# Second attention: VectorE adds GpSimd's pair sums once more; loads, normalising and table loads moved in the other stages

## What is computed

```python
x = x + attn_a(layernorm(x))   # 16 heads of 8, RoPE, heads mixed before and after the softmax
x = x + ffn(layernorm(x))      # 64 of 1024 tokens a sequence, picked by a router, go through a small block
x = x + attn_b(layernorm(x))   # 8 heads of 32, keys and values from a latent of 64
x = x + ffn(layernorm(x))

def attn_b(x):
    q = (x @ Wq.T); kv = x @ Wkv_down.T; k = kv @ Wk_up.T; v = kv @ Wv_up.T
    scores = einsum('bqhd,bkhd->bhqk', q, k) * 32 ** -0.5
    return einsum('bhqk,bkhd->bqhd', softmax(scores), v) @ Wo.T
```

## Time and profile before

| what | us |
|---|---|
| runs of the kernel (three) | 2303.29, 2316.74, 2319.06 |
| the profiled execution's own time | 2306.53 |
| its span, first to last instruction | 2304.7 |
| PE (TensorE matmuls) busy | 2070.8 (90%) |
| DVE (VectorE) busy | 1921.1 (83%) |
| ACT (ScalarE) busy | 1727.7 (75%) |
| POOL (GpSimd) busy | 874.3 (38%) |

### The profile page before, as it was taken

The page is one execution under the profiler, slowest core; times in us unless marked ns, Lnnn a source line. Parts: engine busy times, 40 slices in busy tenths (PEclk is TensorE's granted clock), DMA queues, the critical chain, the costliest instruction groups (busy, mean ns, idle before and its releaser), DMA issues. The chain is left out here.

```text
span 2304.7 us, 61585 instructions
## 1 busy us (share of the span) xinstructions
PE 2070.8 (90%) x24624; PEld 1439.3 (62%) x24624; DVE 1921.1 (83%) x2625; ACT 1727.7 (75%) x3059; POOL 874.3 (38%) x952
## 2 busy tenths in 40 slices
PE   5799999999999999999999999846679999999555
PEld 3477776777777777767777777644336666556454
DVE  6899999999999999999999999683658888888564
ACT  1699998999999899999999999522447777777322
POOL 3433232333332332323233233440028777777230
PEclk9999999999999999999999999956879999999866
DMA  2599999999999999999999999700221111110101
GB/s 100 97 193 197 196 194 194 193 199 193 195 197 195 195 195 195 193 195 193 194 196 199 190 197 195 127 27 0 90 91 31 30 30 33 34 30 23 37 1 37
DMA packets 1099199, 305.39 MB, mean 133 GB/s; under 512 B 1070753, under 2 KB 1092129, under 8 KB 1098657
## 3 DMA queue, kind: packets, MB, share of 16 engines
q1 hardware_dynamic: 1097760, 297.83, 74.6%
q10 hardware_dynamic: 1152, 3.62, 0.4%
HBM read 22.44 MB, written 10.49 MB: 14 GB/s over the span
## 5 line engine op out<-in xcount | busy, mean ns | idle before, releaser
L439 DVE SCALAR_TENSOR_TENSOR a_parts<-a_probs,a_parts 128x1024 f16<-128x1024 f32 x512 | 658.6, 1286 | 70.7 <-ACT a_parts L391 70.1
L350 PE MATMUL a_out_ps<-a_vs,a_pT 128*128 128x128 f16 x4096 | 712.3, 219 | 4.4 <-DMA a_pT<-a_parts 4.4
L354 PE MATMUL a_out_ps<-a_vs,a_pT 128*128 128x128 f16 x4096 | 712.2, 219 | 0.0
L352 PE MATMUL a_out_ps<-a_vs,a_pT 128*128 128x128 f16 x4096 | 712.2, 219 | 0.0
L383 ACT ACTIVATE a_probs<-a_score_ps,a_negmax 128x1024 f32<-128x1024 f32 x512 | 571.2, 1116 | 95.0 <-DVE a_negmax L433 86.6
L433 DVE TENSOR_REDUCE a_negmax<-a_score_ps 128x1 f32<-128x1024 f32 x512 | 621.6, 1214 | 12.2 <-PE a_score_ps L336 9.2
L493 POOL TENSOR_TENSOR a_weighed<-a_own_out,wpost 128x256 f32<-128x256 f32 x256 | 246.6, 963 | 956.5 <-DVE a_parts L439 951.6
L391 ACT ACTIVATE a_parts<-a_probs 128x1024 f16<-128x1024 f32 x512 | 540.2, 1055 | 25.7 <-DMA a_pT<-a_parts 25.1
L350 PEld LDWEIGHTS a_out_ps<-a_vs,a_pT 128*128 128x128 f16 x4096 | 400.7, 98 | 64.4 <-ACT a_own_out L401 4.0
L352 PEld LDWEIGHTS a_out_ps<-a_vs,a_pT 128*128 128x128 f16 x4096 | 400.7, 98 | 59.5
L332 PE MATMUL a_score_ps<-kh,a_qs 128*128 128x512 f16 x1024 | 390.2, 381 | 36.8 <-ACT a_probs L383 28.4
(11 more groups left out here) (199 smaller groups left out, 2217.6 us busy)
## 6 DMA issues: line engine op xcount, KB each, us to landing
a_pT<-a_parts SPq DMA_TRANSPOSE x512, 5.0
b_qs<-q_parts SPq DMA_DIRECT2D x96, 64.0 KB, 1.9
b_ks<-k_parts SPq DMA_DIRECT2D x96, 64.0 KB, 2.0
q_parts<-b_parts SPq DMA_DIRECT2D x32, 128.0 KB, 1.8
k_parts<-b_parts SPq DMA_DIRECT2D x32, 128.0 KB, 1.9
x<-x_dram SPq DMA_DIRECT2D x4, 512.0 KB, 11.9
a_rope<-rope_dram ACTq DMA_DIRECT2D x1, 2048.0 KB, 11.1
out_dram<-x SPq DMA_DIRECT2D x4, 512.0 KB, 5.3
```

What stands on the lines that cost most here:

```text
L350: pe.matmul(out[:, 0:D], hi, vs[:, b, 0, j, :], start=j == 0, stop=False, skip_group_check=True)
L352: pe.matmul(out[:, 0:D], hi, vs[:, b, 1, j, :], start=False, stop=False, skip_group_check=True)
L354: last = pe.matmul(out[:, 0:D], lo, vs[:, b, 0, j, :], start=False, stop=j == JB - 1, skip_group_check=True)
L439: dve.scalar_tensor_tensor(out=parts[:, T % RING_P, 1, :], in0=probs[:, T % RING_P, :], scalar=PSCALE, in1=parts[:, T % RING_P, 0, :], op0 ...
```

## The change

Six edits. (1) attend_b: a new tile quads; VectorE adds pair sums 0 and 1 (half 0) and 2 and 3 (half 1) of a unit, TensorE's ones products read the two results, so they are half as many. The sum of half 1 of unit u-1 stands first in VectorE's unit u, that of half 0 of unit u behind invert(u-1). GpSimd's pair sums wait for VectorE's sum two units before instead of for the products. (2) prepare_a: rope and wpost are loaded by SP behind x, TensorE no longer waits for them; VectorE normalises 8 tiles, ScalarE 24, four in each chunk. (3) The feed stages' weights and tables are loaded once, in project_a (class FeedWeights, held to the end), and no stage waits for them. (4) A square root of one column is taken by ScalarE at the start of project_a and project_b and at the end of the first picked_block. (5) picked_block: hnT is copied ahead of twice. (6) prepare_b: VectorE normalises 8 tiles first and four more behind each chunk's low parts.

```diff
@@ prepare_a @@
+        shift, shift_ready, normed_rest = st.sb(s, "a_shift", [P, NT]), st.sem("a_shift_ready"), st.sem("a_normed_rest")
-        LOADS = 8
+        LOADS = 6
...
                              io["x"][b].rearrange("(t p) d -> p t d", p=P)).then_inc(x_in[b], 16)
+            sp.dma_start(rope[:], io["rope"]).then_inc(rope_in, 16)
+            sp.dma_start(wpost[:], io["wpost"].broadcast_to([P, HA * D])).then_inc(wpost_in, 16)
...
-            act.dma_start(rope[:], io["rope"]).then_inc(w_in, 16)
             act.dma_start(wpre[:], io["wpre"]).then_inc(w_in, 16)
-            act.dma_start(wpost[:], io["wpost"].broadcast_to([P, HA * D])).then_inc(w_in, 16)
             layernorm_scalar(act, ln)
+            act.wait_ge(shift_ready, 1)
             for c in range(NCH + 2):
                 if c < NCH:
                     act.wait_ge(transposed, c + 1)
                     act.copy(hT[:, c * CH:(c + 1) * CH], tps[c % 2][:]).then_inc(hT_ready, 1)
+                if c + DVE_NORMED < NCH:
+                    for t in range(4 * (c + DVE_NORMED), 4 * (c + DVE_NORMED) + 4):
+                        act.activation(xn[:, t, :], x[:, t, :], ACT.Identity, bias=shift[:, t:t + 1],
+                                       scale=ln.rstd[:, t:t + 1]).then_inc(normed_rest, 1)
...
-            normalise(dve, ln, x)
+            dve.scalar_tensor_tensor(out=shift[:], in0=ln.mv[:, :, 0], scalar=-1.0, in1=ln.rstd[:], op0=ALU.mult,
+                                     op1=ALU.mult).then_inc(shift_ready, 1)
+            normalise(dve, ln, x, range(4 * DVE_NORMED))
             dve.wait_ge(w_in, 16 * LOADS)
+            dve.wait_ge(rope_in, 16)
@@ attend_b @@
+        quads = st.sb(s, "b_quads", [P, 2, 2, HALF])
...
-                pe.wait_ge(added, PAIRS * u + 2 * half + 2)
-                for pair in range(2 * half, 2 * half + 2):
-                    for t in range(TILES):
-                        last = pe.matmul(out_ps[t * HDB:(t + 1) * HDB, 0, P:], ones[:],
-                                         sums[:, u % 2, pair, t * P:(t + 1) * P], start=False,
-                                         stop=pair == PAIRS - 1, skip_group_check=True)
+                pe.wait_ge(quad_ready, 2 * u + half + 1)
+                for t in range(TILES):
+                    last = pe.matmul(out_ps[t * HDB:(t + 1) * HDB, 0, P:], ones[:],
+                                     quads[:, u % 2, half, t * P:(t + 1) * P], start=False, stop=half == 1,
+                                     skip_group_check=True)
                 last.then_inc(pv_done, 1)
...
+            def add_pairs(u, half):
+
+                if u < 0:
+                    return
+                dve.wait_ge(added, PAIRS * u + 2 * half + 2)
+                if u >= 2:
+                    dve.wait_ge(pv_done, 2 * (u - 2) + half + 1)
+                dve.tensor_tensor(quads[:, u % 2, half, :], sums[:, u % 2, 2 * half, :], sums[:, u % 2, 2 * half + 1, :],
+                                  ALU.add).then_inc(quad_ready, 1)
+
...
             for u in range(units):
+                add_pairs(u - 1, 1)
                 row_max(TILES * (u + 1) + 2)
                 row_max(TILES * (u + 1) + 3)
                 row_max(TILES * (u + 2))
                 invert(u - 1)
+                add_pairs(u, 0)
                 row_max(TILES * (u + 2) + 1)
+            add_pairs(units - 1, 1)
             invert(units - 1)
...
                 if u >= 2:
-                    pool.wait_ge(pv_done, 2 * (u - 2) + pair // 2 + 1)
+                    pool.wait_ge(quad_ready, 2 * (u - 2) + pair // 2 + 1)
@@ project_a @@
+        @block.sync
+        def _(sp):
+            for to, source in fw.sources:
+                sp.dma_start(to[:], source).then_inc(feed_in, 16)
+            sp.wait_ge(feed_in, 16 * len(fw.sources))
...
         def _(act):
+            act.wait_ge(w_in, 48)
+            act.activation(fw.warm[:], ident[:, 0:1], ACT.Sqrt)
@@ route @@
-        @block.sync
-        def _(sp):
-            sp.dma_start(wr[:], io["w_router"].broadcast_to([P, D])).then_inc(w_in, 16)
...
             add_eps(dve, ln)
+            dve.tensor_reduce(wsum[:], wr[:], AX.X, ALU.add, negate=True).then_inc(summed, 1)
             done = invert_root(dve, ln, 0)
...
-            dve.wait_ge(w_in, 64)
-            dve.tensor_reduce(wsum[:], wr[:], AX.X, ALU.add, negate=True).then_inc(summed, 1)
@@ picked_block @@
+            act.copy(hnT[:], A[:, 0:2 * QK].rearrange("p (r t) -> p r t", r=2)).then_inc(hnT_kept, 1)
             act.copy(twice[:], A[:, 0:2 * QK].rearrange("p (b t) -> p b t", b=NB)[:, :, None, :]
                      .broadcast_to([P, NB, 2, CAP])).then_inc(twice_kept, 1)
-            act.copy(hnT[:], A[:, 0:2 * QK].rearrange("p (r t) -> p r t", r=2)).then_inc(hnT_kept, 1)
...
+            if lnext:
+                act.activation(wts.warm[:], ident[:, 0:1], ACT.Sqrt)
@@ prepare_b @@
-            normalise(dve, ln, x)
+            normalise(dve, ln, x, range(8))
...
+                if c + 2 < NCH:
+                    normalise(dve, ln, x, range(4 * c + 8, 4 * c + 12))
@@ project_b @@
+        @block.scalar
+        def _(act):
+            act.activation(fw.warm[:], fw.ident[:, 0:1], ACT.Sqrt)
```

More of the change, by code:

```diff
@@ L32 @@
 GT_RING = 4
+DVE_NORMED = 2
 LN_EPS, RMS_EPS = 1e-5, 1e-6
@@ L125, in invert_root, with normalise @@
     return n + 5
-def normalise(dve, w, x):
-    for t in range(NT):
+def normalise(dve, w, x, tiles):
+    for t in tiles:
         dve.tensor_scalar(w.xn[:, t, :], x[:, t, :], w.mv[:, t, 0:1], w.rstd[:, t:t + 1],
@@ L208, in _ @@
                 if c < NCH:
-                    pe.wait_ge(ln.normed, 4 * c + 4)
+                    if c < DVE_NORMED:
+                        pe.wait_ge(ln.normed, 4 * c + 4)
+                    else:
+                        pe.wait_ge(normed_rest, 4 * (c - DVE_NORMED) + 4)
                     if c >= 2:
@@ L250, in _ @@
                                              op1=ALU.mult).then_inc(prod_ready, 1)
+            dve.wait_ge(wpost_in, 16)
         @block.gpsimd
@@ L779, in __init__, with project_a @@
         self.loaded = st.sem("pa_w_in")
-def project_a(st, x, acc, pw, lstats):
+def project_a(st, x, acc, pw, lstats, fw):
     nc = st.nc
@@ L846, in _, with route @@
             tile_moments(dve, lstats, taken, NCH - 1)
-def route(st, io, w, tag, x, xn, oh, ohT, xsel, xh, lstats):
+def route(st, w, tag, x, xn, oh, ohT, xsel, xh, lstats):
     nc = st.nc
@@ L855, in route @@
         ln = LnWork(st, s, tag + "ln", xn, lstats)
-        ident = st.sb(s, tag + "ident", [P, P])
-        wr = st.sb(s, tag + "wr", [P, D])
-        iota = st.sb(s, tag + "iota", [P, 2, 2 * CAP])
-        below = st.sb(s, tag + "below", [P, P])
+        ident, wr, iota, below = w.ident, w.wr, w.iota, w.below
         junk = st.sb(s, tag + "junk", [P, 4, P])
@@ L880, in route @@
         block = s.enter_context(nc.Block())
-        @block.sync
-        def _(sp):
-            sp.dma_start(wr[:], io["w_router"].broadcast_to([P, D])).then_inc(w_in, 16)
-            sp.dma_start(iota[:], io["iota"]).then_inc(w_in, 16)
-            sp.dma_start(below[:], io["below"]).then_inc(w_in, 16)
-            sp.dma_start(ident[:], io["ident"]).then_inc(w_in, 16)
-            for to, source in w.sources:
-                sp.dma_start(to[:], source).then_inc(w.loaded, 16)
         @block.scalar
@@ L987, in _ @@
         def _(pe):
-            pe.wait_ge(w_in, 64)
             pe.wait_ge(score_ready, 1)
@@ L1050, in _, with __init__ @@
             turn(NB - 1)
-class BlockWeights:
-    def __init__(self, st, stack, io, tag):
+class FeedWeights:
+    def __init__(self, st, stack, io):
         def sb(name, shape):
-            return st.sb(stack, tag + name, shape)
-        self.ident, self.g, self.wqkv = sb("ident2", [P, P]), sb("g", [P, 2, D]), sb("wqkv", [P, 3, D])
+            return st.sb(stack, "fw_" + name, shape)
+        self.ident, self.g, self.wqkv = sb("ident", [P, P]), sb("g", [P, 2, D]), sb("wqkv", [P, 3, D])
         self.wout, self.w12, self.w3 = sb("wout", [P, D]), sb("w12", [P, 2, 3 * P]), sb("w3", [P, 3, D])
         self.headm, self.pairm, self.causal = sb("headm", [P, HA]), sb("pairm", [P, D]), sb("causal", [P, CAP])
-        self.loaded = st.sem(tag + "w2_in")
-        self.sources = ((self.ident, io["ident"]), (self.g, io["g"].broadcast_to([P, 2, D])),
+        self.wr, self.iota, self.below = sb("wr", [P, D]), sb("iota", [P, 2, 2 * CAP]), sb("below", [P, P])
+        self.warm = sb("warm", [P, 1])
+        self.sources = ((self.ident, io["ident"]), (self.wr, io["w_router"].broadcast_to([P, D])),
+                        (self.iota, io["iota"]), (self.below, io["below"]),
+                        (self.g, io["g"].broadcast_to([P, 2, D])),
                         (self.wqkv, io["fqkv_T"]), (self.wout, io["fout_T"]), (self.w12, io["w12_T"]),
@@ L1295, in _, with feed_forward @@
                 last.then_inc(put_done, 1)
-def feed_forward(st, io, tag, x, lstats, lnext):
```

(10 more changed lines are left out.)

18 lines of the change are left out of this document (7 added, 11 removed).

## The result

| | before | after |
|---|---|---|
| time, median (lowest to highest) | 2310.93 us (2303.29 to 2319.06, 4 runs) | 2507.02 us (2505.49 to 2507.65, 4 runs) |
| span of the profiled execution | 2304.7 us | 2505.5 us |
| granted TensorE clock, mean | 0.946 | 0.915 |

What follows compares the result with a forecast made beforehand. It took a ring through VectorE's new sum in the second attention, 8.86 us a unit, as the bound: 2304.7 + 123 - 8.5 - 5.1 = 2414.1 of span, 2416 us in time, range 2346 to 2445.

Steps and rivals of the forecast that it cites:

- Second attention, +123: attend_b: 60 units growing from 6.84 to 8.86 us, 121 us, plus about 1.2 and 0.6 us at the end.
- The ring: attend_b: half 1's sum delays a row maximum, TensorE, the next exponentials and so its own next inputs; 8.86 us a unit.
- collision: attend_b: VectorE's sum of half 1 waits for GpSimd's next pair sum on the shared SBUF port; 1.00 us a unit.
- the rival: attend_b: VectorE's sum doesn't wait for GpSimd's pair sum; unit 7.86 us, +63 us, total 2356; chance 0.17.
- the rival on the granted clock: attend_b: TensorE's idle time drops it to half clock; 12.8 us units, a quarter of 60 adding 59 us, 2475; chance 0.12.
- the likeliest case: Whole kernel: 2416 us, own range 2400 to 2430, attend_b units of 8.86 us at clock 1.00; chance 0.66.
- the 3.45 us of the ring: attend_b: from L586 through scores, exponentials and scaled maxima to the next exponential 6, 3.45 us a unit at full clock.
- the units could alternate: attend_b: by the skill's loop that falls to the low clock every round, units could alternate between clocks; no size given.
- The second sum: attend_b: VectorE's sum of half 0, behind the reciprocal, costs nothing; up to 1 us if it met a GpSimd sum.
- Loads and normalising, -8.5: Ahead of the first attention: statistics end near 13 us, 9.1 earlier, less 0.2 and 0.3; bounds -5 and -9.5.
- Small stages, -5.1: Feed stages and projections: table loads -1.7 and +0.5, router weights' DMA wait -2.9, later copy -1.0.
- The wait for the root: Both feed stages: VectorE's 2.3 us wait behind the table load falls to about 0.3 each, -1.7 over both.

Runs made afterwards that it cites:

- experiment 3: Changed kernel plus 18 unread 256-column matmuls filling TensorE's idle stretch in each unit of the second attention: 2419.46 us, ratio 1.0461.
- experiment 2: Changed kernel, but GpSimd's first pair sum of a unit waits until VectorE's sum of half 1 of the unit before is done: 2353.8 us, ratio 1.019.
- experiment 7: Changed kernel with first row maximum ahead of half 1's sum: 2296.77 us; same with old prepare_a: 2306.61; changed kernel with old attend_b: 2293.89.
- e2: The kernel before with only the changed attend_b: 2514.4 us, ratio 1.0884.
- e11: Changed kernel with the next unit's first row maximum ahead of the sum of half 1, and prepare_a as before the change: 2306.61 us, ratio 0.9979.
- experiment 4: Changed kernel plus unread matmuls in TensorE's idle stretch, fewer than 18: with 7, 2418.89 us, ratio 1.0452; with 3, 2488.49 us, one run.
- e6: Changed kernel, first row maximum ahead of the sum of half 1, and GpSimd's next pair sum waiting for that sum: 2296.15 us, ratio 0.992.

## Why the prediction was right in direction and wrong in size

- **Second attention, +123.** The ring, with collision and at full clock, was measured by experiment 3: its attend_b lasts 572.2 us (1697.9 to 2270.1) against 452.7, so +119.5. Without the collision (experiment 2) it is 2197.5 - 1692.1 = 505.4, so +52.7, where the rival had 63. These two terms stood.
- **The step that failed is the rival on the granted clock:** "if a quarter of 60 units ran so, 15 x 3.9 = 59 us more", with a chance of 0.12, and ahead of it granted clock 1.00 in the likeliest case. The clock falls in 59 of 60 units. A fall doesn't make a unit 12.8 us long, either: it slows the 3.45 us of the ring behind the idle stretch to 4.77 and is over before the next round. The unit is 10.24 - 8.86 = 1.38 us longer than forecast, in 60 units 83 us; by the stages it is 659.5 - 572.2 = 87.3. This is the miss but for 4 us: 2416 + 87 = 2503 against 2507.
- Why the reading failed: the earlier trace rows show a stretch with 36.9 of 45 us busy and clock 1.00, and the prediction saw that 28% of idle time went beyond its 18%, and still gave the low clock 0.12 and a quarter of the units. It was the one price for which no row of before stood near, and the range should have reached across it. The mark that could be seen beforehand is the place: TensorE's idle stretch lies on the ring, so whatever slows TensorE behind it lengthens the next round too.
- **The page on the clock** was nearer than the sum. The Trainium skill, "TensorE: Matmul & The Clock Gate", section "HAM oscillation — how this bites in real kernels", describes a clock that falls in every round of a loop because of its wait. The changed kernel's rows agree in kind (1.01 us in place of 0.60 in nearly every unit), but behind a wait for VectorE of 2.25 us, shorter than the 3 to 5 us of the page's example. The prediction's reading of it, that the units could alternate, isn't borne out: they fall one after the other.
- **Collision.** The rule of the Trainium skill, "SBUF — State Buffer", section "SBUF: two separate sides", held for a sum beside a sum: 1.74 us against 0.69 (experiment 2), going 0.14 us ahead of GpSimd's recorded end, as the earlier trace rows had it for L439. The second sum was costed at nothing, and 0.63 us shows it.
- **Loads and normalising, -8.5.** The statistics end at 10.76 + 3.38 = 14.14 us instead of 22.16, so 8.0 us earlier. The prediction said near 13 and 9.1, a slip in its own sum: x near 11 and 3.19 us of statistics make 14.2. The first attention starts 9.2 us earlier in this pair of executions, 7.8 in the mean of experiment 7's count, and the medians there differ by 9.8. The size of the term held. The counterpart of the earlier trace rows:

```profile
10.76 3.38 DVE L106 BATCH_NORM_STATS2 lna_stats<-x 128x6 f32<-128x128 f32 x16 [0.58 <-DMA x<-x_dram]
```

- **Small stages, -5.1.** The counterparts of the earlier trace rows:

```profile
L123 DVE RECIPROCAL f_ln_r<-f_ln_sd 128x32 f32<-128x32 f32 x2 | 0.7, 352 | 0.6 <-ACT f_ln_sd L149 0.6
L941 DVE TENSOR_REDUCE f_wsum<-fw_wr 128x1 f32<-128x128 f32 x2 | 0.6, 279 | 0.0
L149 ACT ACT_TABLE_LOAD x1 | 1.3, 1283 | 3.9 <-issue 3.9
```

  The wait for the root is 0.6 in place of 2.3 (-1.7, as forecast) and the wait for the DMA is gone. The first feed stage gained 8.0 us in this pair of executions; it took 124.7 in e2, which has none of these edits, and 119.8 to 122.4 in the eleven other traces of kernels that have them, so 3 us or more of the 8.0 belong to before's single execution. The second feed stage shows none of the 2.8 us forecast for it (half of 1.7, half of 2.9, and 0.5): 124.4 us before, 124.3 after, 124.6 in e2, and 121.6 to 125.0 in the eleven others. All edits outside attend_b together: -10.4 us in the first comparison (2298.89 against 2309.23), -15.8 in the second (2293.89 against 2309.71); forecast -13.6. The sum held; how it is shared out among the small stages isn't shown.
- **attend_a, +12.2, forecast 0.** No edit touches it. From the first to the last query scaling it takes 1355.0 us in before and 1366.0 in after, but also 1362.8 in e2 and 1364.4 in e11, which keep the old preparation, and 1361.2 to 1369.6 in the ten others. Before's profiled execution is the quickest of them all; most of the difference isn't the change's.

## What to carry to other kernels

Free time of an engine says little about whether it can take more work; where the new instruction stands in that engine's queue decides. Ask what waits behind it and whether it closes a ring with its own producer: here one line moved behind one row maximum is worth 213 us. And when an edit makes TensorE idle in one piece in each round, price the low clock on the path behind that piece as a case of its own, at the full number of rounds.

## What the runs showed of the hardware that wasn't expected

- A wait of TensorE of 2.16 or 2.25 us in a unit of 10.24 us is followed by the low clock in 59 of 60 units, one of 1.83 or 1.93 us (3 matmuls, experiment 4) in 44 of 60, a wait of 1.21 us (experiment 2) or 1.49 us (7 matmuls) in none. Work without use, 7 matmuls of 0.93 us together, makes the kernel 88 us faster (2418.9 against 2507.0).
- The collision works the other way round too: in e6 VectorE's sum and GpSimd's pair sum start within 0.03 us of each other, and GpSimd's is the one that takes 1.80 us in place of 1.27. GpSimd's record begins first there, but it overlaps the end of the instruction ahead of it, so its start is rough:

```profile
1906.95 0.46 POOL L788 TENSOR_TENSOR oT<-b_kept,b_inv 128x128 f32<-128x128 f32 x1
...
1907.37 1.80 POOL L780 TENSOR_TENSOR b_sums<-b_probs 128x512 f32<-128x512 f32 x1
1907.40 0.63 DVE L754 TENSOR_TENSOR b_quads<-b_sums 128x512 f32<-128x512 f32 x1
```

  GpSimd's ends at 1909.17; had it got going 1.27 before that, this was at 1907.90, 0.13 ahead of the end of VectorE's sum (1908.03). So here too one waits for the other, rather than both running slower.
